# Choices sorted by expert number, early gathers of the lower rows, and a turned sequence ahead of two whole experts

## Chip, cores and metric

One core of one Trainium2 chip runs the kernel. The metric is the device time of one execution in microseconds; of the kernel before, three runs gave 588.18 us (median), 587.75 and 590.46 us.

## What is computed

The reference is a chain of two layers over 16 sequences of 256 tokens with 256 features, all in float32. Layer 0 (attention with a conditioning bias, then a top-1 mixture of 8 experts) fills the first half of the kernel and is not touched by the change. Layer 1 has two parts, and the change is in how they meet:

```python
scores = softmax(logits); topk_w, topk_idx = top_k(scores, 2)      # per token, 8 small experts
y_all = einsum('etm,emh->eth', leaky(x @ w_gate) * (x @ w_up), w_down)
y = (y_all[topk_idx] * topk_w[..., None]).sum(1) + shared_expert(x)
...
pooled = y.mean(axis=1); gates = softmax(top-2 of pooled @ gate_w.T + gate_b)   # per sequence, 8 experts
out = x + einsum('be,beso->bso', gates, gelu(einsum('bsd,eod->beso', y, expert_w) + expert_b))
```

## The kernel before

Only the second half matters here. It has three stages that hand over to one another.

**Choice tiles.** The 8192 pairs of token and chosen expert are sorted by expert into 71 tiles of 128 rows (`TILES2`), every expert starting on a new tile. POOL gathers a tile's token rows by an indirect DMA (`choice_rows`), PE turns, multiplies and turns back (`choice_in`, `choice_up`, `choice_turn`, `choice_down`, three tiles in flight), ACT and DVE empty the banks, and SP stores the result to the DRAM tensor `y2_dram` (the profile calls it `y_sorted`), counted by three semaphores `c_st`. In DVE's queue each turn of the loop over `TILES2 + LAG` holds a copy of the turned tile (L2856) and two products (L2860, L2862).

**Shared expert.** Behind the last tiles PE works off the last units of the shared expert (L1503, L1520) while the stores land.

**Sequences.** For each of the 16 sequences POOL gathers four blocks of 128 rows out of `y2_dram`: two halves (`NB` = 2) times the token's first and second choice, by the row numbers `pos_k_i`. All go through `gather_rows` (L917), and behind each stands `space()`, a memset that POOL waits for (L947). The destination `yk` has three buffers (`RT`), so the gathers of sequence b wait for the sum of sequence b-3. No gather may start until all 71 tiles are stored (`c_st`). DVE then adds the weighted rows to the shared result (`sum_choices`, four instructions of L2883), PE turns the sum (`turn_z`, L1642), ACT copies it and gets its pooled mean, PE multiplies it by the gate weights (`gate_logits`, L1656), DVE picks the two experts (`gates`, L2892 to L2898), and PE reads their numbers into registers (`experts_of`, a load of `d_top`). For each of the two experts PE issues a bias (`gated_bias`, L1663) and eight matmuls (two calls of `gated` with four instructions each, L1669); ACT applies gelu (L2032) and DVE weighs the result into `res` (L2915), which SP stores.

PE's order in that stage is written out in `gated_step`: turn sequence b, second half of sequence b-1's first expert, gate logits of b, all of b-1's second expert, then the numbers of b and the first half of its first expert. At the last sequence one half of the second expert is drawn ahead of the turn, and `last_choice` splits the end in two. DVE's own `gated_step` has the gate chain of b, then the first weighing of b-1, then the sum of b+1.

## Time and profile before

| | us |
|---|---|
| median of three runs | 588.18 |
| the profiled execution | 589.62 |
| its span in the profile | 587.9 |
| mean granted TensorE clock | 0.998 of full speed |
| PE busy | 558.1 (95%) |
| DVE busy | 321.1 (55%) |
| ACT busy | 243.1 (41%) |
| POOL busy | 233.9 (40%) |

Busy time is the sum of an engine's instructions over the whole span; the matmul row counts pipelined instructions, whose ends are modelled, so a busy PE isn't one at its peak. Which engine sets the end is read by stage: from the chain of waits, from the windows of the three stages, and from what stands behind "idle before" in the timeline.

### The profile page before, as it was taken

The page shows a single profiled execution, that of the slowest core. Times are in us where ns is not written, and L with a number is a line of the kernel's source. Part 1 is how long each engine was busy: PE and PEld are TensorE (multiplying, and loading weights), DVE is VectorE, ACT ScalarE, POOL GpSimd, SP SyncE. Part 2 cuts the span into 40 slices and gives each one's busy share as a digit, 9 for nine tenths or more (in the row PEclk, how much of TensorE's full clock was granted, in tenths as well). Part 3 has the DMA queues.
Part 4 walks back from the last instruction along what each step waited for, and adds up shares of the span by engine and source line. Part 5 has one row for each costly group of instructions (what it writes and reads, how often), then busy time and mean ns, then how long its engine had stood idle before and what let it go on. Part 6 is the DMA issues. An engine that isn't in the chain of part 4 may idle for free.

```text
span 587.9 us, 11468 instructions
## 1 busy us (share of the span) xinstructions
PE 558.1 (95%) x3816; PEld 463.4 (79%) x3816; DVE 321.1 (55%) x967; ACT 243.1 (41%) x670; POOL 233.9 (40%) x319
## 2 busy tenths in 40 slices
PE   7999999988999999999999989999999998998886
PEld 4788887744999999988888968888878887776664
DVE  3877758676322225733538754444444344666665
ACT  1555444660211111116544245555555454443432
POOL 2312211042111121007546365555555078777860
PEclk9999999999999999999999999999999999999999
DMA  5960000186995522513395035565655322444441
GB/s 149 387 284 4 1 1 2 64 366 254 325 345 191 184 68 73 153 64 74 76 308 191 0 100 148 160 159 150 161 153 153 96 78 85 136 129 121 127 134 56
DMA packets 48853, 83.96 MB, mean 143 GB/s; under 512 B 8946, under 2 KB 41587, under 8 KB 47252
## 3 DMA queue, kind: packets, MB, share of 16 engines
q1 hardware_dynamic: 40676, 60.97, 29.7%
q0 software_dynamic: 8112, 22.16, 15.5%
q8 instruction: 36, 0.59, 0.4%
q14 instruction: 29, 0.24, 0.1%
HBM read 62.25 MB, written 20.84 MB: 141 GB/s over the span
## 4 chain that ended last, share of the span: by engine, by line
PE 70%; POOL 12%; DVE 5%; issue 5%; DMA 4%; ACT 2%; another core or an unknown queue 0%; SPq 0%; POOLq 0%; DVEq 0%; ACTq 0%
POOL arena L917 10%; PE psum L1331 10%; PE psum L1344 9%; PE psum L1591 9%; PE psum L1503 7%; PE psum L1605 5%; PE psum L1187 5%; PE psum L1159 5%; PE psum L1520 3%; PE psum L1583 3%; DMA arena<-x,row_tok 3%; POOL iota_i L947 2%; PE psum L1167 2%; PE psum L1538 1%; PE psum L1181 1%
## 5 line engine op out<-in xcount | busy, mean ns | idle before, releaser
L917 POOL DMA_INDIRECT arena<-x,row_tok x71 | 68.1, 959 | 55.7 <-PE psum L1583 47.2
L917 POOL DMA_INDIRECT arena<-y_sorted,pos_k_i x64 | 65.3, 1021 | 35.2 <-issue 16.1
L1591 PE MATMUL psum<-big_w,arena 128*128 x284 | 72.9, 379 | 0.0
L1927 ACT ACTIVATE arena<-psum,arena 128x128 f32<-128x128 f32 x64 | 18.2, 368 | 106.5 <-PE psum L1331 85.0
L1669 PE MATMUL psum<-big_w,arena 128*128 x248 | 61.3, 379 | 0.0
L1331 PEld LDWEIGHTS psum<-arena,big_w 128*128 128x128 f32 x512 | 59.5, 192 | 1.7 <-issue 1.0
L1331 PE MATMUL psum<-arena,big_w 128*128 128x128 f32 x512 | 59.8, 275 | 0.8 <-DVE arena L2624 0.8
L1503 PE MATMUL psum<-arena,big_w 128*128 128x256 f32 x256 | 59.9, 381 | 0.2 <-ACT arena L1946 0.2
L1591 PEld LDWEIGHTS psum<-big_w,arena 128*128 128x128 f32 x284 | 53.7, 190 | 7.2
L1344 PE MATMUL psum<-arena 128*128 128x256 f32 (+1 forms) x256 | 57.7, 379 | 0.0
L2860 DVE SCALAR_TENSOR_TENSOR arena<-arena 128x128 f32<-128x128 f32 x71 | 20.8, 293 | 62.2 <-ACT arena L2013 62.2
L1503 PEld LDWEIGHTS psum<-arena,big_w 128*128 128x128 f32 x256 | 47.3, 190 | 7.1 <-ACT arena L1946 0.9
L1344 PEld LDWEIGHTS psum<-arena 128*128 128x128 f32 x256 | 47.5, 190 | 5.8
L1669 PEld LDWEIGHTS psum<-big_w,arena 128*128 128x128 f32 x248 | 45.7, 190 | 6.7
L917 POOL DMA_INDIRECT arena<-h_late,row_tok x16 | 15.3, 959 | 81.7 <-PE psum L1319 69.6
L1605 PE MATMUL psum<-big_w,arena 128*128 x142 | 44.1, 392 | 1.3 <-ACT arena L2010 1.3
L892 POOL TENSOR_TENSOR arena<-arena 128x512 f32<-128x512 f32 x16 | 19.0, 1191 | 59.9 <-DVE arena L2223 59.8
L2010 ACT COPY arena<-psum 128x256 f32<-128x256 f32 x71 | 26.4, 372 | 22.2 <-PE psum L1605 19.5
L1187 PE MATMUL psum<-arena 128*128 128x256 f32 x144 | 32.7, 380 | 0.4 <-ACT arena L1806 0.4
L1159 PE MATMUL psum<-arena 128*128 128x128 f32 x256 | 32.6, 289 | 0.0
L1520 PE MATMUL psum<-big_w,arena 128*128 128x256 f32 x128 | 30.6, 382 | 1.3 <-ACT arena L1950 1.3
L1159 PEld LDWEIGHTS psum<-arena 128*128 128x128 f32 x256 | 31.4, 204 | 0.3 <-DVE arena L2223 0.2
(338 smaller groups left out, 997.8 us busy)
## 6 DMA issues: line engine op xcount, KB each, us to landing
y_sorted<-arena SPq DMA_DIRECT2D x71, 128.0 KB
big_w<-w SPq DMA_DIRECT2D x8, 1024.0 KB, 5.3
tokens<-x SPq DMA_DIRECT2D x4, 1024.0 KB, 13.3
x<-tokens SPq DMA_DIRECT2D x16, 256.0 KB, 2.6
out<-arena SPq DMA_DIRECT2D x15, 256.0 KB
y_late<-arena SPq DMA_DIRECT2D x16, 128.0 KB, 1.7
big_w<-expert_w_t SPq DMA_DIRECT2D x1, 2048.0 KB, 7.4
arena<-x,row_tok POOLq DMA_INDIRECT x71
```

The source lines that it names most:

```text
L917: pool.indirect_dma_start(dst, None, rows, bass.IndirectOffsetOnAxis(ap=idx, axis=0)).then_inc(done, 16)
L1159: mm = pe.matmul(bank[a][:, (j % 4) * P:(j % 4 + 1) * P], wq_s[:, k, j * P:(j + 1) * P], xt_l[:, k, :], start=k == 0, stop=k == KD - 1)
L1187: mm = pe.matmul(bank[6][:, 0:D], lhs(j), wo_s[:, j, :], start=j == 0, stop=j == NPAIR - 1)
L1331: mm = pe.matmul(bank[1 + 2 * u + f // 4][:, (f % 4) * P:(f % 4 + 1) * P], big_w[:, c:c + P], g_t[u][:, k, :], start=k == 0, stop=k == KD - 1)
L1344: mm = pe.matmul(bank[5 + j % 2][:, 0:D], act_t[j % 2][:, f, :], arena[:, bass.ds(e * (NF * D) + f * D, D)], start=f == 0, stop=f == NF - 1)
L1503: mm = pe.matmul(bank[up_bank(b) + q][:, half * S:(half + 1) * S], w[:, k, q * M1:(q + 1) * M1], p_s[:, unit(b)[1][k], :], start=k == 0, s ...
L1520: mm = pe.matmul(bank[6][:, n * D:(n + 1) * D], mid[u][q][:, n * P:(n + 1) * P], md_s[:, E1 + q, :], start=q == 0, stop=q == NSH - 1)
L1591: mm = pe.matmul(bank[2 + i % RT][:, 0:2 * M1], c_gt[i % RT][:, k, :], mgu_s[:, k, bass.ds(e, 1), :].rearrange("p a m -> p (a m)"), start= ...
L1605: pe.matmul(bank[5][:, 0:D], c_midt[i % RT], md_s[:, bass.ds(e, 1), :].rearrange("p a d -> p (a d)"), start=True, stop=True).then_inc(c_dn, 1)
L1669: mm = pe.matmul(o, z_t[u][:, k, n * P:(n + 1) * P], ew_s[:, k, bass.ds(e, 1), :].rearrange("p a d -> p (a d)"), start=False, stop=n == NB ...
L2010: act.copy(c_y[t % RT], bank[5][:, 0:D]).then_inc(c_yc, 1)
L2860: dve.scalar_tensor_tensor(c_mid[v], c_leak[v], 0.01, c_leak[v], ALU.mult, ALU.max).then_inc(c_lkd, 1)
```

## The change

It has four parts.

1. **By expert number.** At tile 12 of the choice loop DVE runs `by_expert`, 14 small instructions. They order a token's two choices by row number (and so by expert number, since experts are stored one behind the other), rewrite `pos_k_i` and the weights `w_k` in that order, and work out how many tiles of each of the three store semaphores lie before the last expert's first tile.
2. **Lower rows early.** The lower row of a token never lies in the last expert's tiles. POOL waits, behind all its choice gathers, for the stores up to that expert only, and gathers the lower rows of the first five sequences (`y_lo`, 5 buffers). Then come the full wait and the higher rows of three sequences (`y_hi`, 3 buffers); from there on two blocks of higher rows of b and two of lower rows of b+2 alternate. There are 64 gathers as before.
3. **A turned sequence ahead.** PE's step now turns sequence c+1, reads the numbers of c, does all of its first expert, the gate logits of c+1, and all of its second expert. The special order at the last sequence goes, apart from `last_choice`. DVE's step sums sequence b+1 ahead of the gate chain of b.
4. **Filled destination.** SP copies 71 x 128 rows of x into `y2_dram` in three DRAM to DRAM transfers, queued behind the first load of the layer-0 weights, and waits for them before the first store of a choice tile.

The diff, cut to its core:

```diff
-        yk = [N.take(2 * NB, D) for _ in range(RT)]
+        y_hi = [N.take(NB, D) for _ in range(RT)]
...
+        NLO = 5
+        y_lo = [N.take(NB, D) for _ in range(NLO)]
...
+            def fill_choice():
+                for r0 in range(0, TILES2 * P, T):
+                    n = min(T, TILES2 * P - r0)
+                    sp.dma_start(y2_dram[r0:r0 + n, :], x[0:n, :]).then_inc(filled, 16)
...
                 sp.dma_start(big_w[:, :], w1).then_inc(ld_w1, 16)
+                fill_choice()
...
+            sp.wait_ge(filled, 16 * NFILL)
             for i in range(TILES2):
                 sp.wait_ge(c_yc, i + 1)
...
+            pool.wait_ge(table, 4)
+            for u in range(RT):
+                hold(pool, c_st[u], pool.value_load(stores_i[0:1, u:u + 1], min_val=16, max_val=16 * len(range(u, TILES2, RT))))
+            for b in range(NLO):
+                low_rows(b)
             for u in range(RT):
                 pool.wait_ge(c_st[u], 16 * len(range(u, TILES2, RT)))
+            for b in range(RT):
+                high_rows(b)
+            for b in range(RT, B):
+                pool.wait_ge(d_z, b - RT + 1)
+                high_rows(b)
+                if b + NLO - RT < B:
+                    low_rows(b + NLO - RT)
...
+            def gated_step(c):
+
+                u, v = c % RT, (c + 1) % RT
+                more = c + 1 < B
+                if more:
+                    turn_z(c + 1, v)
+                first, second = experts_of(c, u)
+                gated_bias(c, 0, first)
+                gated(c, u, 0, 0, first)
+                gated(c, u, 0, 1, first)
+                if more:
+                    gate_logits(c + 1)
+                    gated_bias(c, 1, second)
+                    gated(c, u, 1, 0, second)
+                    gated(c, u, 1, 1, second)
+                else:
+                    last_choice(c, u, second)
...
+            def by_expert():
+
+                for u in range(RT):
+                    g = dve.tensor_scalar(first_i[:, u:u + 1], tstart2[:, E1 - 1:E1], float(RT - 1 - u), 21846.0, ALU.add, ALU.mult)
+                link(dve.tensor_tensor(lower, pos_k[:, :, 0], pos_k[:, :, 1], ALU.is_lt))
+                link(dve.tensor_scalar(first_i, first_i, 16, None, ALU.logical_shift_right))
+                dve.tensor_copy(first_f, first_i)
+                link(dve.tensor_scalar(higher, lower, -1.0, 1.0, ALU.mult, ALU.add))
+                dve.tensor_scalar(stores_i[:, :], first_f, 1.0, 16.0, ALU.max, ALU.mult)
+                dve.tensor_tensor(pos_k_i[:, :, 0], pos_k[:, :, 0], pos_k[:, :, 1], ALU.min)
+                link(dve.tensor_tensor(pos_k_i[:, :, 1], pos_k[:, :, 0], pos_k[:, :, 1], ALU.max))
+                dve.sem_inc(table, 1)
+                dve.tensor_tensor(w_lo, w_k[:, :, :], lower.unsqueeze(1).broadcast_to([P, 2, NC]), ALU.mult)
+                link(dve.tensor_tensor(w_hi, w_k[:, :, :], higher.unsqueeze(1).broadcast_to([P, 2, NC]), ALU.mult))
+                dve.tensor_tensor(w_k[:, 0, :], w_lo[:, 0, :], w_hi[:, 1, :], ALU.add)
+                dve.tensor_tensor(w_k[:, 1, :], w_lo[:, 1, :], w_hi[:, 0, :], ALU.add)
+
+            SORT_AT = 12
...
+                if i == SORT_AT:
+                    by_expert()
...
+                if b + 1 < B:
+                    all_of(sum_choices(b + 1, (b + 1) % RT, (b + 1) // RT))
                 chain = gates(b, b % RT) if b < B else iter(())
                 for _ in range(3):
                     next(chain, None)
-                if 1 <= b:
-                    outs[b - 1] = weigh(b - 1, (b - 1) % RT, (b - 1) // RT)
-                    next(outs[b - 1])
-                if 1 <= b and b + 1 < B:
-                    all_of(sum_choices(b + 1, (b + 1) % RT, (b + 1) // RT))
+                outs[b - 1] = weigh(b - 1, (b - 1) % RT, (b - 1) // RT)
+                next(outs[b - 1])
                 next(chain, None)
```

**POOL, where the choice gathers end.** Before, the first gather of `y_sorted` waits for all three store semaphores:

```order
L917 DMA arena<-x,row_tok 128x256 [waits c_g] x64
L917 DMA arena<-y_sorted,pos_k_i 128x256 [waits c_st2,c_st1,c_st0]
L947 MEMSET iota_i 128x128
L917 DMA arena<-y_sorted,pos_k_i 128x256 [waits paced]
L947 MEMSET iota_i 128x128
```

Changed (here `gather_rows` is L937 and the memset L967):

```order
L937 DMA arena<-x,row_tok 128x256 [waits c_g] x64
L1020 TENSOR_LOAD stores_i [waits table]
L1020 ISA x2
L1020 TENSOR_LOAD stores_i [waits c_st0]
L1020 ISA x2
L1020 TENSOR_LOAD stores_i [waits c_st1]
L1020 ISA x2
L937 DMA arena<-y_sorted,pos_k_i 128x256 [waits c_st2]
L967 MEMSET iota_i 128x128
L937 DMA arena<-y_sorted,pos_k_i 128x256 [waits paced]
L967 MEMSET iota_i 128x128
```

Three reads of `stores_i` now stand there, each with a partial wait for a store semaphore behind it. Ten gathers with their memsets follow, and only then the wait for all stores (`c_st1,c_st2,c_st0,paced`) that stood alone before.

**PE, one step of the sequence stage.** Before (L1642 turns, L1669 is an expert's matmuls, L1663 a bias, L1656 the gate logits, L1311 the load of the expert numbers; the ISA rows set up addresses):

```order
L1311 TENSOR_LOAD d_top [waits d_ok]
L1663 ISA [waits d_ge]
L1663 MATMUL psum<-big_w,ones_bf 128x512
L1669 ISA
L1669 MATMUL psum<-big_w,arena 128x256
L1669 ISA
L1669 MATMUL psum<-big_w,arena 128x256
L1642 MATMUL psum<-ident,arena 128x128 [waits d_ztc,d_z]
L1642 MATMUL psum<-ident,arena 128x128 x3
L1669 MATMUL psum<-big_w,arena 128x256 x2
L1656 MATMUL psum<-big_w,arena 128x8 [waits d_log,d_ztc]
```

Changed (the same four are L1675, L1702, L1696 and L1689, the load L1344):

```order
L1675 MATMUL psum<-ident,arena 128x128 [waits d_ztc,d_z]
L1675 MATMUL psum<-ident,arena 128x128 x3
L1344 TENSOR_LOAD d_top [waits d_ok]
L1696 ISA [waits d_ge]
L1696 MATMUL psum<-big_w,ones_bf 128x512
L1702 ISA
L1702 MATMUL psum<-big_w,arena 128x256
L1702 ISA
L1702 MATMUL psum<-big_w,arena 128x256 x3
L1689 MATMUL psum<-big_w,arena 128x8 [waits d_log,d_ztc]
```

The load of the numbers has moved behind the turn of the next sequence, and between the turn and the gate logits there are now the bias and all four matmuls of an expert instead of two matmuls (each counts as two instructions in the profile, so eight and four there).

**DVE, one step of the sequence stage, changed.** L2918 is the sum, L2927 to L2933 the gate chain, L2950 the weighing:

```order
L2918 SCALAR_TENSOR_TENSOR arena<-arena,w_k 128x256 [waits a_dc,d_lo4,d_zt]
L2918 SCALAR_TENSOR_TENSOR arena<-arena,w_k 128x256
L2918 SCALAR_TENSOR_TENSOR arena<-arena,w_k 128x256 [waits d_z1,c_got1]
L2918 SCALAR_TENSOR_TENSOR arena<-arena,w_k 128x256
L2927 SCALAR_TENSOR_TENSOR arena<-psum,arena 128x8 [waits d_lg]
L2930 MAX arena<-arena 128x8 [waits d_log]
L2933 MAX_INDEX d_top<-arena 128x8 [waits d_sub]
L2950 SCALAR_TENSOR_TENSOR arena<-arena,tokens 128x512 [waits d_gt,d_ge]
```

The sum stood behind the first weighing and waited once, for four gathers; it now stands ahead of the gate chain and waits for the lower rows first and for the higher rows (`c_got`) in its middle.

## Rows read from the trace of the kernel before

**Rows 1.** The page: the chain that ended last, by engine and by line.

```profile
PE 70%; POOL 12%; DVE 5%; issue 5%; DMA 4%; ACT 2%; another core or an unknown queue 0%; SPq 0%; POOLq 0%; DVEq 0%; ACTq 0%
```

**Rows 2.** Windows of sequence stage: stretch, length, busy per engine, clock, DMA share, GB/s.

```profile
core 0: us, PE busy (x) PEld busy (x) DVE busy (x) ACT busy (x) POOL busy (x), PEclk, DMA share, GB/s
499.00:575.00 76.00, 68.27 (x344) 51.83 (x344) 50.27 (x161) 31.29 (x104) 56.48 (x91) 1.00 0.42 125
```

**Rows 3.** Timeline of POOL: start, duration, instruction, idle before; the gathers' end.

```profile
454.93 0.94 POOL L917 DMA_INDIRECT arena<-x,row_tok  x1 [0.73 <-PE psum L1583]
470.87 0.94 POOL L917 DMA_INDIRECT arena<-y_sorted,pos_k_i  x1 [15.00 <-DMA y_sorted<-arena]
471.82 0.22 POOL L947 MEMSET iota_i<- 128x128 int32 x1
472.31 0.95 POOL L917 DMA_INDIRECT arena<-y_sorted,pos_k_i  x1 [0.27 <-POOL iota_i L947]
...
501.17 0.95 POOL L917 DMA_INDIRECT arena<-y_sorted,pos_k_i  x1 [0.27 <-POOL iota_i L947]
...
569.24 0.98 POOL L917 DMA_INDIRECT arena<-y_sorted,pos_k_i  x1 [0.27 <-issue]
```

**Rows 4.** The chain in order of time: from a gather to the sum.

```profile
563.37 2.66 DMA arena<-y_sorted,pos_k_i
```

**Rows 5.** Timeline, the first two sums and PE's first expert.

```profile
478.91 1.79 DVE L2883 SCALAR_TENSOR_TENSOR arena<-arena,w_k 128x256 f32<-128x256 f32 x4
490.24 1.82 DVE L2883 SCALAR_TENSOR_TENSOR arena<-arena,w_k 128x256 f32<-128x256 f32 x4
492.68 0.10 PEld L1663 LDWEIGHTS psum<-big_w,ones_bf 128*128 128x128 bf16 x1
```

**Rows 6.** Timeline of PE and its weight loads, one step.

```profile
558.64 0.38 PE L1663 MATMUL psum<-big_w,ones_bf 128*128 x1
560.58 0.38 PE L1663 MATMUL psum<-big_w,ones_bf 128*128 x1
562.50 0.42 PEld L1642 LDWEIGHTS psum<-ident,arena 128*128 128x128 f32 x4 [1.07 <-DVE arena L2883]
564.08 0.52 PEld L1656 LDWEIGHTS psum<-big_w,arena 128*128 128x128 f32 x4 [0.46 <-ACT arena L2019]
564.55 0.38 PE L1663 MATMUL psum<-big_w,ones_bf 128*128 x1
```

**Rows 7.** One choice tile on DVE and PE.

```profile
422.96 0.28 DVE L2856 COPY arena<-psum 128x128 f32<-128x128 f32 x1
423.78 0.30 PEld L1605 LDWEIGHTS psum<-big_w,arena 128*128 128x128 f32 x2
```

**Rows 8.** Timeline of DVE: small instructions in a chain, and two without a wait.

```profile
311.78 0.16 DVE L2795 TENSOR_SCALAR cnt_i<-arena 128x8 int32<-128x8 f32 x1
312.80 0.42 DVE L2800 SCALAR_TENSOR_TENSOR arena<-arena 128x256 f32<-128x256 f32 x1
...
315.53 0.65 DVE L2805 TENSOR_SCALAR arena<-pos_k_i 128x64 int32<-128x64 int32 x1
```

**Rows 9.** SP's issues and landing time of the first weight load; what follows on the queue.

```profile
13.59 1.44 SPq L721 DMA_DIRECT2D big_w<-w  x1
111.23 0.29 SPq L725 DMA_DIRECT2D h_late<-arena  x1
big_w<-w SPq DMA_DIRECT2D x1, 28.0
```

**Rows 10.** Window between the first weight load and the next transfer, columns as in Rows 2.

```profile
45.00:111.00 66.00, 64.27 (x726) 52.84 (x725) 48.74 (x102) 33.57 (x69) 10.92 (x10) 1.00 0.01 2
```

**Rows 11.** The load of the expert numbers: duration ns min/median/max.

```profile
L1311 PEldq TENSOR_LOAD <-d_top x16: 532/534/547, 491.1 to 577.9; - x16
```

**Rows 12.** Timeline of the end, on PE and DVE.

```profile
574.80 0.57 PEld L1642 LDWEIGHTS psum<-ident,arena 128*128 128x128 f32 x4
577.19 0.17 DVE L2892 SCALAR_TENSOR_TENSOR arena<-psum,arena 128x8 f32<-128x8 f32 x1 [2.29 <-PE psum L1656]
577.67 0.16 DVE L2898 FIND_INDEX8 d_top<-arena 128x8 uint32<-128x8 f32 x1
578.57 0.10 PEld L1663 LDWEIGHTS psum<-big_w,ones_bf 128*128 128x128 bf16 x1 [0.86 <-issue]
```

More of the change, by code:

```diff
@@ L408, in bass_adaln_ffn_kernel @@
         tile_f2 = Q.take(TILES2)
+        first_i = Q.take(RT).bitcast(I32)
+        first_f = Q.take(RT)
+        stores_i = sb("stores_i", [P, RT], I32)
+        lower = Q.take(NC)
+        higher = Q.take(NC)
+        w_lo = Q.take(2, NC)
+        w_hi = Q.take(2, NC)
         NLB = NU // 4
         lgt_2 = Q.take(S)
+        assert N.at <= E0 * NF * D + Q.at
         wt_g = router_g
@@ L534, in bass_adaln_ffn_kernel @@
         d_back = sem("d_back")
-        d_pos = sem("d_pos")
         d_log = sem("d_log")
@@ L553, in bass_adaln_ffn_kernel @@
         c_st = [sem(f"c_st{k}") for k in range(3)]
-        d_got = [sem(f"d_got{k}") for k in range(3)]
+        d_lo = [sem(f"d_lo{k}") for k in range(NLO)]
+        filled = sem("filled")
         d_st = [sem(f"d_st{k}") for k in range(3)]
@@ L567, in bass_adaln_ffn_kernel @@
         half_st0 = 16 * len(range(0, TILES2, RT))
-        last_got = c_got[0:2]
-        last_got0 = [16 * len(range(u, TILES2, RT)) for u in range(2)]
+        d_hi, d_hi0 = c_got, [16 * len(range(u, TILES2, RT)) for u in range(RT)]
+        NFILL = -(-TILES2 * P // T)
         l_rows_ev, l_beat_g, ld_rest = ld_x[2], ld_x[1], ld_x[3]
@@ L721, in _ @@
                 sp.dma_start(big_w[:, :], w1).then_inc(ld_w1, 16)
+                fill_choice()
                 late_rows = h_late[1:, :].rearrange("(c p) d -> p c d", p=P)
@@ L1732, in _ @@
                 shared_down(s, s % 2)
-            first_expert(0, 0)
-            for b in range(1, B + 1):
-                gated_step(b)
+            for c in range(B):
+                gated_step(c)
             def every_expert(b, first):
@@ L2868, in sum_choices @@
                     hold(dve, d_zt, b - RT + 1)
-                split = isinstance(b, int) and b == B - 1
-                if split:
-                    dve.wait_ge(last_got[0], last_got0[0] + 32)
-                else:
-                    hold(dve, d_got[u], 64 * turn_no + 64)
+                dve.wait_ge(d_lo[b % NLO], 32 * (b // NLO) + 32)
                 if isinstance(b, int):
```

59 lines of the change are left out of this document (17 added, 42 removed).

## The prediction

> **What bounds the kernel now.** I read the chain of waits first, then the windows, then the timelines of the stage that the change is in. Over the whole span the chain lies 70% on PE and 12% on POOL [rows 1]. POOL's part is one stage: with the choice tiles done, each sequence costs four gathers, and in the window of the sequences POOL is busy 56.48 of 76 us though nothing it does is long [rows 2]. The timeline of POOL says why: a gather takes 0.95 us, then comes a memset of 0.22 and 0.27 of hand-over, so the next one starts 1.44 us later (472.31 behind 470.87) at best. All 64 run from 470.87 to 569.24 + 0.98 = 570.22, 99.35 us or 1.55 each [rows 3]. Four are 6.2 us per sequence.
>
> PE needs less. In one step the bias and eight matmuls of an expert take 560.58 - 558.64 = 1.94 us, the four transposes about 0.42, the gate logits 564.55 - 564.08 = 0.47 [rows 6]. Two experts, a turn and the logits: 4.8 us. The step takes 564.55 - 558.64 = 5.91, and the rest stands in the same rows as idle time: 1.07 us for DVE's sum, which waits for gathers, and 0.46 for ACT's copy of the turned sequence [rows 6]. So gathers bound the stage, PE stands a good microsecond behind. Ahead of it POOL is idle for 15.00 us, from its last choice gather to the landing of the last store [rows 3].
>
> **The sum, part by part,** in the time of the profiled execution (589.62, of which 587.9 is the span).
>
> *Fill.* 71 x 128 rows of 1 KB are 9.3 MB. The transfers stand behind a load of 8.4 MB that is issued at 13.59 and needs 28.0 us, 0.30 MB per us; at that rate the fill ends near 42 + 31 = 73. SP's next transfer is issued at 111.23 [rows 9], and in between the DMA engines are at 0.01 [rows 10]. Cost 0: the cover is 38 us of spare time. No row shows a DRAM to DRAM copy. Were each byte counted twice (read and written) at the same rate, it would end at 42 + 62 = 104, still in time; that is why I take 0, with a rival below for less.
>
> *by_expert.* 14 instructions of 32 to 64 elements per partition or fewer. Five small chained ones take 312.80 - 311.78 = 1.02 us, 0.20 each [rows 8]. Six of the 14 are waited for (6 x 0.20), the others overlap and start about 0.1 apart: 2.0 us, and I take 2.3. If every one cost what the slow one of the same chain does, 0.65 [rows 8], it would be 9; if they fell into DVE's gaps, 0. In the tile loop PE is the bound, and what queues behind the block on DVE is the copy of a turned tile, done at 422.96 + 0.28 = 423.24 while PE begins its matmul at 423.78 [rows 7]. That leaves 0.54 us of cover, so PE loses 2.3 - 0.54 = 1.8 us, once, and nothing later gives it back. **+1.8.**
>
> *Lower rows early.* Ten gathers at 1.45 need 14.5 us and fit in the hole of 15.00, if the partial wait is over by then. It is: counting the reference's choices for these inputs gives 69 used tiles, of which the last expert has the last 11, so POOL waits for tile 57, stored some ten tiles ahead of 455.9. At 470.87 POOL goes on with six gathers of higher rows (to about 480), then with the first block of two and two behind the sum of sequence 0, done at 478.91 + 1.79 = 480.7 [rows 5]; by 487 it has issued 20. Now a new wait comes: the next block needs the sum of sequence 1, which DVE's order puts at 490.24 + 1.82 = 492.06 [rows 5]. So POOL stands idle for 5 us, and the head start isn't ten gathers: gather 21 starts at 492.2 instead of 501.17 [rows 3]. That idle time also means that the early gathers may be 5 us late for nothing. From gather 21 on POOL waits for nothing (its next waits are for sums three sequences back), and the remaining 44 take what the last 44 take now, 570.22 - 501.17 = 69.05 us [rows 3]. They end at 561.3. **-8.9.**
>
> *PE's new order.* PE's first expert starts at 492.7 as before [rows 5]. At 4.85 us a step PE would begin the turn of sequence 15 at 492.7 + 14 x 4.85 = 560.6; the gathers are later, so they still decide at the end. A gather lands 2.66 us after its start [rows 4], 1.7 after its end; with DVE's queue I take 2.1. The higher rows of sequence 14 are complete two gathers ahead of the last (558.2), land at 560.3, and the two halves of the sum that wait for them take 0.9: 561.2. The turn comes at 561.4. Then a wait that wasn't there: DVE has the gate chain of 13 behind this sum (577.83 - 577.19 = 0.64 us [rows 12]), PE loads the numbers (0.53 [rows 11]), and starts the expert's weights 578.57 - 577.83 = 0.74 after the chain [rows 12]: 562.7, though the turn was done at 561.9. Expert, logits, expert: 562.7 + 1.94 + 0.47 + 1.94 = 567.05, where sequence 15 (summed by 564.4) is turned. Today the turn comes at 574.80 [rows 12], 4.6 us behind the last gather; then it is 5.8 behind. **+1.2.**
>
> *The end.* Behind the turn of sequence 15 PE now has eight matmuls and two biases more (10 x 0.215 = 2.15 us), since nothing is drawn ahead; two waits go, 0.46 for the copy, as in every step [rows 6], and 0.86 for the numbers [rows 12]. **+0.9.**
>
> Sum: 1.8 - 8.9 + 1.2 + 0.9 = -5.0, so 584.6 for the profiled execution. The median is 1.44 lower than that execution, and the predicted median is 588.18 - 5.0 = **583.2**.
>
> *Rule:* the time of the load that moved behind the turn is a row here, 0.53 us from SBUF. The Trainium skill (Runtime: NRT & Kernel Launch, The launch sequence) gives 1.3 us for such a load from HBM; by that figure the one exposed load would add 0.8 and the median be 584.0. The trace's 0.53 decides.
>
> **Rivals.**
> 1. *PE becomes the bound.* The pace of 1.55 holds stretched gathers; the plain pace is 1.44, and 44 x 1.44 = 63.4 us ends at 555.6. Then PE's floor of 560.6 for the last turn decides, 6.4 earlier than above: 576.8. For it: most gathers do take 0.95. Against: DVE's sums stay as dense as now. Halfway is likelier than the whole: 577 to 580.5. Chance 0.17.
> 2. *The numbers come late in every step.* DVE now sums b+1 ahead of the gate chain of b. If sums wait for gathers throughout, each step has the 0.8 us wait: 14 x 5.65 = 79.1, last turn at 571.8, 4.7 later than above, a median of 587.9. It decides from the point where the gathers have no lead over PE. Against: POOL starts three to five sequences ahead and loses about 1.3 us a step, so the lead lasts past half of the stage. Chance 0.14.
> 3. *Slower: the fill is still running at 111.* It decides below 9.3 MB in 69 us, 0.135 MB per us, under half the rate of the load ahead. SP's stores of the attention result then stand behind it, and PE's next work behind them; at 0.10 MB per us the end is 135, 24 us late, less 5 gained: 607. Against: 64 rows of 64 KB, the row length of that load. Chance 0.04.
> 4. *DVE's block costs 9 us* (upper bound above), PE 8.5: 589.9. Chance 0.04.
> 5. *The early gathers do nothing,* because the partial wait is as late as the full one. POOL then ends as before, and the new order alone gives +1.8 + 1.2 + 0.9: 592. Chance 0.03.
>
> **How the numbers follow.** The forecast has 0.58; its own bounds (block 0.5 to 3, gathers 1.45 to 1.62) reach from 579 to 587. A measurement tells apart some 0.5%, 2.9 us. Faster by more: nearly all of the forecast (0.56), rival 1 (0.17) and a little of rival 2 (0.03), 0.76. Within 0.5%: the rest of these two and half of rival 4, 0.15. Slower: 0.09. The range reaches down through most of rival 1 and up through rival 2: 578.0 to 588.3.
>
> **What would show it.** Right: ten gathers of `y_sorted` between 456 and 472 in the shifted time; POOL idle for some 5 us ahead of gather 21; PE steps near 4.85 us with no wait for the copy in the first half, near 6 in the last; the wait for numbers only there; one gap of near 1.8 us on PE around tile 12; no stretch ahead of 111 longer. Wrong: idle time ahead of the bias in every step (rival 2), POOL waiting for `d_z` throughout (rival 1), a late store at 111 (rival 3).

## The result and the profile after

The changed kernel takes 590.25 us (median of 19 runs, 587.65 to 596.55); the kernel before, on the same chip, 587.75 (19 runs). The ratio is 1.006, interval 1.0041 to 1.0079: slower by 0.6%, where 0.8% faster was forecast. Ratios, here and below, are taken over all runs of both kernels, so they aren't exactly those of the medians; and since the kernel before takes 586.27 to 590.46 us by the chip, only ratios compare runs of different chips. The profiled executions are 593.32 and 589.62, spans 591.6 and 587.9, so 3.7 us are to be found.

From the page of the changed kernel, the clock and traffic in 40 slices of 14.8 us, and the chain that ended last [rows 1]:

```profile
PEclk9998899999999999999999999999999999999999
...
GB/s 149 389 423 353 135 2 1 2 206 428 190 330 269 191 139 52 137 113 47 90 185 336 6 45 144 136 156 160 159 161 161 150 126 55 115 144 131 119 117 56
...
PE 72%; POOL 9%; DVE 7%; issue 5%; DMA 4%; ACT 1%; SPq 1%; POOLq 0%; DVEq 0%; ACTq 0%
```

POOL's share of the chain fell from 12% to 9%, as it should. But "issue", an engine that waits for nothing the profile shows, stands at 5%, and PE's clock is below 0.9 in slices 4 and 5 alone, the last two with the fill's traffic. So the program has to be cut into stages, at marks that both kernels have: SP's store of the attention result, POOL's last choice gather, its last gather, the end.

| stretch | before | after | difference | forecast |
|---|---|---|---|---|
| start to attention store | 111.23 | 120.45 | +9.2 | 0 |
| to the last choice gather | 343.70 | 343.55 | -0.2 | +1.8 |
| to the end of the last gather | 115.29 | 107.59 | -7.7 | -8.9 |
| to the end of the span | 17.68 | 20.01 | +2.3 | +2.1 |

The loss lies in the first stretch, hundreds of microseconds ahead of anything that the change was about. Only the fill is new there. SP's timeline of the changed kernel and, from the view of transfers, issue to landing:

```profile
15.19 1.85 SPq L698 DMA_DIRECT2D y_sorted<-x  x3
...
120.45 0.29 SPq L744 DMA_DIRECT2D h_late<-arena  x1
```

```profile
y_sorted<-x SPq DMA_DIRECT2D x1, 896.0 KB, 52.2
...
y_sorted<-x SPq DMA_DIRECT2D x2, 44.2
```

The fill has landed by 15.19 + 1.85 + 52.2 = 69 us at the latest, earlier than the 73 that I gave it; nothing queues behind it. PE's timeline, before and changed, and the windows of that stretch (columns as in [rows 2]):

```profile
17.50 0.69 PE L1167 MATMUL psum<-arena 64*64 64x65 f32 x32 [0.69 <-ACT arena L1839]
...
53.08 0.69 PE L1167 MATMUL psum<-arena 64*64 64x65 f32 x32 [0.73 <-issue]
```

```profile
16.51 0.70 PE L1200 MATMUL psum<-arena 64*64 64x65 f32 x32 [0.88 <-DVE arena L2312]
...
56.21 1.15 PE L1200 MATMUL psum<-arena 64*64 64x65 f32 x32 [4.86 <-issue]
...
58.83 1.93 PE L1214 MATMUL psum<-arena 64*64 64x512 f32 x8
...
66.33 1.58 PE L1192 MATMUL psum<-arena 128*128 128x128 f32 x12 [2.22 <-issue]
```

The first of these windows is the kernel before, the other three are the changed one:

```profile
50.00:55.00 5.00, 4.26 (x85) 3.35 (x87) 1.19 (x3) 2.07 (x5) 0.00 (x0) 1.00 0.02 7
```

```profile
50.00:55.00 5.00, 1.35 (x11) 1.02 (x9) 0.00 (x0) 1.45 (x3) 0.00 (x0) 0.90 1.17 397
55.00:60.00 5.00, 3.79 (x74) 2.44 (x74) 2.52 (x4) 1.01 (x3) 0.16 (x1) 0.50 1.11 341
45.00:111.00 66.00, 58.63 (x669) 48.45 (x667) 39.03 (x72) 26.75 (x55) 10.71 (x9) 0.92 0.30 100
```

PE stands idle for 4.86 and 2.22 us with no semaphore to blame. At the first place the kernel before waits too, but 0.73 us. Behind the changed kernel's wait the clock is at 0.50, the 1.2 GHz level, and the eight matmuls of L1214 take 1.93 us, 1.04 elsewhere. Idle time is (4.86 - 0.73) + 2.22 = 6.4 us. The slow clock costs more than the 2.8 that this leaves of the 9.2: PE was 1.0 us ahead at the start (16.51 for 17.50), and from where PE resumes to the store it takes 120.45 - 56.21 = 64.2 us where the kernel before takes 111.23 - 53.08 = 58.1, so 6.1 more, of which 2.22 is the second wait. The slow clock is the other 3.9: 6.4 + 3.9 - 1.0 is 9.2 but for rounding. The last row answers to [rows 10]: 669 matmul records in place of 726.

What is PE waiting for? The DMA view lists a queue that I had passed over, the one that brings instructions. Cut to 0.2 us (columns: packets, MB, share of 16 engines), it shows one block of 0.02 MB (16 KB) at a time. Before, at 50.4, and after, at 53.2:

```profile
q8 instruction: 1, 0.02, 29.0%
```

```profile
q1 hardware_dynamic: 2, 0.13, 193.9%
q8 instruction: 1, 0.02, 34.6%
```

The block itself takes hardly longer (29% and 35% of 16 x 0.2 us, some 1 us). It is later, and PE goes on 2.7 to 3.0 us behind it in both: 50.4 to 53.08, 53.2 to 56.21. The second wait has its block too: the changed kernel's next one is at 63.6, and PE goes on at 66.33, 2.7 us behind. The view doesn't say whose instructions q8 brings; that these blocks are PE's is concluded from this distance, which all profiles below have. The Trainium skill (Runtime: NRT & Kernel Launch, Instruction fetch mechanics) says that a sequencer fetches its program in 16 KiB blocks over a DMA queue of its own, at a cost "mostly hidden". The trace agrees on the block and its queue; hidden it is in the kernel before, but for 0.73 us, and not here.

The late stages, POOL first:

```profile
466.61 0.95 POOL L937 DMA_INDIRECT arena<-y_sorted,pos_k_i  x1 [1.66 <-DMA y_sorted<-arena]
...
494.82 0.95 POOL L937 DMA_INDIRECT arena<-y_sorted,pos_k_i  x1 [0.27 <-issue]
...
501.84 0.99 POOL L937 DMA_INDIRECT arena<-y_sorted,pos_k_i  x1 [5.85 <-DVE arena L2918]
...
570.64 0.95 POOL L937 DMA_INDIRECT arena<-y_sorted,pos_k_i  x1 [0.27 <-issue]
```

The partial wait costs 1.66 us where the full one cost 15.00 [rows 3], twenty gathers are out by 495.8, POOL then stands for 5.85 us, and the last 44 take 69.75. PE's weight loads, with the idle time ahead of them:

```profile
374.84 0.14 PEld L1632 LDWEIGHTS psum<-ident,arena 128*128 128x128 f32 x1 [1.58 <-issue]
...
506.36 0.58 PEld L1675 LDWEIGHTS psum<-ident,arena 128*128 128x128 f32 x4
...
511.05 0.58 PEld L1675 LDWEIGHTS psum<-ident,arena 128*128 128x128 f32 x4
...
545.93 0.42 PEld L1675 LDWEIGHTS psum<-ident,arena 128*128 128x128 f32 x4 [2.14 <-DVE arena L2918]
547.18 0.10 PEld L1696 LDWEIGHTS psum<-big_w,ones_bf 128*128 128x128 bf16 x1 [0.82 <-issue]
...
572.33 0.42 PEld L1675 LDWEIGHTS psum<-ident,arena 128*128 128x128 f32 x4 [1.98 <-DVE arena L2918]
573.57 0.10 PEld L1696 LDWEIGHTS psum<-big_w,ones_bf 128*128 128x128 bf16 x1 [0.82 <-issue]
577.62 0.58 PEld L1675 LDWEIGHTS psum<-ident,arena 128*128 128x128 f32 x4
```

There is the gap behind by_expert (1.58, or 1.37 counted in PE's matmuls), steps of 4.69 us with no wait in the first half, and from 545.9 on five steps that wait for gathers and then 0.82 for the numbers.

### The profile page after: what moved, and what is told of

It reads as the page before. It is cut to its first block, busy times and chain, and to the rows that moved or that the text cites. A ratio compares the mean times of both kernels' runs of the same rounds, so it can differ in the third digit from the quotient of the medians.

```text
span 591.6 us, 11515 instructions
## 1 busy us (share of the span) xinstructions
PE 556.2 (94%) x3816; PEld 467.4 (79%) x3816; DVE 321.6 (54%) x981; ACT 240.7 (41%) x670; POOL 232.3 (39%) x319
## 4 chain that ended last, share of the span: by engine, by line
PE 72%; POOL 9%; DVE 7%; issue 5%; DMA 4%; ACT 1%; SPq 1%; POOLq 0%; DVEq 0%; ACTq 0%
PE psum L1364 10%; PE psum L1377 9%; PE psum L1536 9%; PE psum L1624 9%; POOL arena L937 8%; PE psum L1220 5%; PE psum L1638 5%; PE psum L1192 4%; PE psum L1553 4%; PE psum L1616 3%; DMA arena<-x,row_tok 2%; PE psum L1200 2%; POOL iota_i L967 2%; PE psum L1702 1%; PE psum L1571 1%
## 5 line engine op out<-in xcount | busy, mean ns | idle before, releaser
L937 POOL DMA_INDIRECT arena<-x,row_tok x71 | 68.1, 958 | 55.5 <-PE psum L1616 45.9
L937 POOL DMA_INDIRECT arena<-y_sorted,pos_k_i x64 | 64.9, 1014 | 28.0 <-issue 13.8
L1624 PE MATMUL psum<-big_w,arena 128*128 x284 | 72.9, 379 | 0.0
L1702 PE MATMUL psum<-big_w,arena 128*128 x248 | 58.6, 379 | 0.0
L1702 PEld LDWEIGHTS psum<-big_w,arena 128*128 128x128 f32 x248 | 46.6, 189 | 5.9
L937 POOL DMA_INDIRECT arena<-h_late,row_tok x16 | 15.4, 960 | 81.7 <-PE psum L1352 69.5
L1638 PE MATMUL psum<-big_w,arena 128*128 x142 | 44.6, 396 | 0.0
L2918 DVE SCALAR_TENSOR_TENSOR arena<-arena,w_k 128x256 f32<-128x256 f32 x64 | 28.1, 480 | 15.9 <-DMA arena<-y_sorted,pos_k_i 14.9
L1220 PE MATMUL psum<-arena 128*128 128x256 f32 x144 | 34.4, 394 | 0.4 <-ACT arena L1826 0.4
```

The lines of the kernel that those rows point to most:

```text
L937: pool.indirect_dma_start(dst, None, rows, bass.IndirectOffsetOnAxis(ap=idx, axis=0)).then_inc(done, 16)
L1220: mm = pe.matmul(bank[6][:, 0:D], lhs(j), wo_s[:, j, :], start=j == 0, stop=j == NPAIR - 1)
L1624: mm = pe.matmul(bank[2 + i % RT][:, 0:2 * M1], c_gt[i % RT][:, k, :], mgu_s[:, k, bass.ds(e, 1), :].rearrange("p a m -> p (a m)"), start= ...
L1638: pe.matmul(bank[5][:, 0:D], c_midt[i % RT], md_s[:, bass.ds(e, 1), :].rearrange("p a d -> p (a d)"), start=True, stop=True).then_inc(c_dn, 1)
L1702: mm = pe.matmul(o, z_t[u][:, k, n * P:(n + 1) * P], ew_s[:, k, bass.ds(e, 1), :].rearrange("p a d -> p (a d)"), start=False, stop=n == NB ...
L2918: m = dve.scalar_tensor_tensor(z_s[u][:, n, :], (y_hi[u] if k else y_lo[b % NLO])[:, n, :], w_k[:, k, bass.ds(b * NB + n, 1)], base, ALU.m ...
```

## The experiments

The theory: the fill holds back the fetch of PE's instructions. Its rivals: the loss is elsewhere; or the traffic as such slows PE.

**e1, the fill alone in the kernel before.**

```diff
                 sp.dma_start(big_w[:, :], w1).then_inc(ld_w1, 16)
+                fill_choice()
...
+            sp.wait_ge(filled, 16 * NFILL)
             for i in range(TILES2):
```

> The kernel before with the fill alone: the same three transfers issued behind the first weight load, SP waiting for them ahead of the first choice store. Theory A (the fill costs what the change lost, and nothing else was mispriced): the gap between 48 and 67 us appears here too, +9.3 us, 597 by the measurement's median of 587.75, ratio 1.016. Theory B (the loss comes from the choice and sequence stages, and the stretched attention stage of the profiled run was an accident): no change, 587 to 589.

Measured: 597.94, ratio 1.0109 (1.0058 to 1.0161). PE waits 6.65 us at the same place, the store comes at 118.75, 7.5 us late. Theory B has fallen: the fill alone makes a loss of that kind. By the ratio it is 6.4 us of 590.46, where 9.3 was expected; PE waits once here, and twice in the changed kernel.

**e2, the change without the fill.** The lower rows are read from 59 of the 71 tiles, which is enough for these inputs.

```diff
-                fill_choice()
...
-                    gather_rows(y_lo[b % NLO][:, n, :], y2_dram, ...)
+                    gather_rows(y_lo[b % NLO][:, n, :], y2_dram[0:59 * P, :], ...)
```

> The changed kernel without the fill (the lower rows are read from the first 59 of the 71 tiles only, which the partial wait covers for these inputs). Theory A: attention as before, 9.3 us off the 590.25 of the changed kernel, so 581 to 583, ratio 0.991 to the kernel before. Theory B: 590 as with the fill.

Measured: 585.97, ratio 0.9913 (0.9884 to 0.9941). Of the 590.46 of the kernel before on that chip the ratio makes 5.1 us, the two medians are 4.5 apart; -5.0 was forecast.

**e3 and e5, the fill in pieces of 4 KB.** e3 puts pairs in the outer dimension (a = 2), e5 sixteen.

```diff
-                    sp.dma_start(y2_dram[r0:r0 + n, :], x[0:n, :]).then_inc(filled, 16)
+                    sp.dma_start(y2_dram[r0:r0 + n, :].rearrange("(b a r) d -> a b (r d)", a=16, r=4),
+                                 x[0:n, :].rearrange("(b a r) d -> a b (r d)", a=16, r=4)).then_inc(filled, 16)
```

> The changed kernel, the same bytes of fill cut into pieces of 4 KB in place of 64 KB. Theory A1 (a block of PE's instructions that is fetched stands behind the fill's long packets on its DMA engine): PE's wait for nothing shown at 51 and 64 us shrinks to under 1 us and the clock stays at 1.00, the total near 582 to 584. Theory A2 (the number of bytes moved, by its share of the memory or by the clock, slows PE): the same loss, 589 to 591, with a clock of 0.5 somewhere while the fill runs.

> The changed kernel, the fill in pieces of 4 KB again, now interleaved over 16 so that all DMA engines carry them, and the bytes move about as fast as in the change (over 250 GB/s between 42 and 70 us). The third run moved 4 KB pieces at 54 GB/s only, over few engines, so it told long packets from short ones at unlike rates. Theory A1 (a fetched block of PE's instructions stands behind long packets): the block that was fetched at 49.8 without the fill and at 53.2 with it is fetched within 0.5 us of its time, PE's wait at 52 is near 1 us, clock 1.00, and the total 582 to 586 if the fill is over by 111. Theory A2 (bytes per us, whatever their packets): the wait of 4 to 6 us and the clock of 0.5 are back, 589 to 592.

Measured, e3: 686.42, ratio 1.1609 (1.1548 to 1.167). SP's timeline and one window tell why:

```profile
15.68 171.40 SPq L698 DMA_DIRECT2D y_sorted<-x  x3
```

```profile
55.00:65.00 10.00, 10.00 (x118) 9.14 (x120) 6.79 (x14) 5.35 (x11) 2.38 (x2) 1.00 0.14 54
```

Issuing takes SP until 187, at 54 GB/s and a share of 0.14 of 16 DMA engines, some two of them. The Trainium skill (DMA: Bandwidth & Descriptors, Why a DMA increments its semaphore by 16 and not by 1) says that a transfer is spread over the largest number up to 16 that divides the sizes of its outermost dimension: two here, as the trace shows. This was my own edit's trap, and by accident it is rival 3 of the prediction, SP's store stuck behind the fill, at 96 us. PE lost nothing in attention up to there (wait 0.74, clock 1.00), but at so low a rate that tells nothing of packets. Hence e5: 587.72, ratio 1.003 (1.0006 to 1.0054). PE's timeline and the windows:

```profile
54.97 1.14 PE L1201 MATMUL psum<-arena 64*64 64x65 f32 x32 [3.90 <-issue]
```

```profile
50.00:55.00 5.00, 1.10 (x13) 0.86 (x11) 0.00 (x0) 1.45 (x3) 0.00 (x0) 0.89 1.03 324
55.00:60.00 5.00, 5.00 (x76) 2.94 (x77) 3.69 (x6) 1.69 (x4) 1.20 (x1) 0.50 1.02 324
```

At full rate short pieces hold the fetch back as well (it stands at 52.0), and PE waits 3.90 us. The idea that only long packets do it has fallen; whether they add something (4.86 us for 3.90), one profile of each doesn't tell.

**e4 and e6, the fill paced**, in 512 and in 1024 rows, one transfer at a time.

```diff
-                for r0 in range(0, TILES2 * P, T):
+                for j, r0 in enumerate(range(0, TILES2 * P, FR)):
+                    sp.wait_ge(filled, 16 * j)
...
                 sp.dma_start(big_w[:, :], w1).then_inc(ld_w1, 16)
+                sp.wait_ge(ld_w1, 16)
                 fill_choice()
```

> The changed kernel, the same bytes in 18 transfers of 512 rows, each issued when the one ahead has landed, the first when the weight load has. Packets keep their kind but few are queued at a time (512 KB over 16 engines). Theory A1: each engine has one packet of the fill ahead of a fetch at most and idle time between transfers, so the waits of PE are under 1 us, total 582 to 584; the fill ends before 111. Theory A2: as many bytes over some 70 us in place of 25: a third of the loss per us for three times as long, so most of the loss stays, 587 to 591.

> The changed kernel, nine transfers of 1024 rows, each issued when the one ahead has landed: 64 KB for each of 16 DMA engines at a time, where the fourth run had 32 KB. Theory A1: a fetch stands behind at most one packet that is under way, 64 KB at some 25 GB/s, 2.6 us, so PE's wait at 52 is anywhere from 1 to 3.5 us, total 583 to 588. If several queued packets had to go first whatever the pacing (A1b), it would be as in the fourth run. Theory A2: a loss by the bytes, 587 to 591.

Measured: e4 587.05, ratio 0.9931 (0.9902 to 0.9959), PE's wait 1.32; e6 587.69, ratio 1.0013 (0.9984 to 1.0042), PE's wait 2.60. In the window 50 to 55 the DMA engines are at 0.61 (213 GB/s) in e6; in e4 at 0.36 (109 GB/s) from 45 to 55. By its ratio e4 would take 587.75 x 0.9931 = 583.7 on the first chip, in the range of theory A1. By these three (e4, e6, e5) the block is later, the more of the DMA engines' time the fill takes. Two more runs say that the share alone doesn't settle it. e8 and e10, further down, have e4's paced pieces. In e8 PE waits 1.25 us with a share of 0.65 in the window 50 to 55; in e10 it waits 2.19 with 0.36, and the clock falls behind it:

```profile
53.31 0.70 PE L1202 MATMUL psum<-arena 64*64 64x65 f32 x32 [2.19 <-issue]
```

What the block meets just when it is due may decide; no run separates that.

**e9, the same fill later.** One wait is added, nothing else:

```diff
                 sp.dma_start(big_w[:, :], w1).then_inc(ld_w1, 16)
+                sp.wait_ge(o_ps, 4)
                 fill_choice()
```

> The changed kernel with its fill as it is (three transfers, long packets, full rate), issued when the fourth product of attention is done, at about 63 us in place of 15. Without the fill PE's blocks are fetched at 41, 49.8, 53, 57, then 68, 78, 89 and 99 us, and only behind the fetch of 49.8 does PE wait. Theory A3 (what the fill delays is the fetch of instructions, by some 3 us while it keeps all DMA engines busy, and that costs only where PE has used up its blocks): from 63 to some 90 us three fetches come late and PE waits for none of them, clock 1.00, the total as without a fill, ratio 0.991 to 0.994. Theory A2' (the fill's traffic slows PE or takes its clock wherever it lies): a loss of 5 to 9 us stays, ratio 1.002 to 1.01.

Measured: 583.41, ratio 0.9896 (0.9856 to 0.9937), clock 1.000 over the span. The windows ahead of the fill and during it:

```profile
42.00:63.00 21.00, 20.09 (x203) 17.21 (x194) 15.52 (x29) 9.45 (x20) 4.76 (x4) 1.00 0.01 3
63.00:93.00 30.00, 30.00 (x390) 25.33 (x389) 21.29 (x39) 16.28 (x35) 6.50 (x6) 1.00 0.94 311
```

PE is busy for all of the 30 us in which the fill runs at 311 GB/s. The blocks do come late (71.4, 84.4 and 93.0 us, without a fill 68.4, 78.6 and 89.0), and PE waits for none. This settles it: the traffic neither slows PE nor takes its clock; it delays fetches, here by 3 to 6 us, and that costs only where three blocks follow each other (49.8, 53, 57): there the changed kernel waits twice, the others of the table once. My reading is that PE has no block in hand there. It goes with the windows: the kernel before has 85 matmuls between 50 and 55, and 38 between 45 and 50. No run shows how many blocks PE holds.

**e13, a load into SBUF in the fill's place.** The first weights are loaded twice; no fill, lower rows as in e2.

```diff
                 sp.dma_start(big_w[:, :], w1).then_inc(ld_w1, 16)
+                sp.wait_ge(ld_w1, 16)
+                sp.dma_start(big_w[:, :], w1).then_inc(ld_w1, 16)
```

> The second run's kernel (no fill) that loads the first weights a second time, 8.4 MB from HBM to SBUF in 64 KB rows, issued when they have landed the first time: from 44 to some 70 us. Theory A4 (any transfer that keeps all 16 DMA engines busy holds back the fetch, whatever its ends): PE's wait at 52 is 3 to 6 us, clock 0.5 behind it, 588 to 592 in all, ratio 1.000 to 1.006. Theory A5 (only a copy from HBM to HBM does it): the wait stays near 1 us, the clock at 1.00, ratio 0.991.

Measured: 589.4, ratio 1.0015 (0.9986 to 1.0044). PE's timeline and the windows:

```profile
56.00 1.15 PE L1199 MATMUL psum<-arena 64*64 64x65 f32 x32 [4.02 <-issue]
```

```profile
50.00:55.00 5.00, 1.99 (x14) 1.57 (x12) 0.00 (x0) 1.45 (x3) 0.00 (x0) 1.00 0.99 423
55.00:60.00 5.00, 4.00 (x75) 2.48 (x75) 2.71 (x4) 1.22 (x3) 0.36 (x1) 0.66 0.97 419
```

An ordinary weight load does the same. The kernel before has one from 14 to 42, with a DMA share of 0.88 between 25 and 40; two blocks are fetched under it, at 22.4 and 34.6, and PE waits for neither, as in e9. It is the time of the transfer that matters, not its kind.

All of it in one table. "Fetch" is the window of 0.2 us that holds the block, "resumes" PE's next matmul, "DMA" the share in the window 50 to 55 (45 to 55 in e1 to e4, 42 to 63 in e9), "clock" that of the window 55 to 60 (55 to 65 in e1 to e4). "Late" corrects for the start, which differs by up to 1.8 us between profiles: it is the block's distance from PE's stop at 16 to 18 us (17.50 before), less 32.93. In the six profiles without a bulk transfer around 50 us whose clock is full at the start (before, e2, e9, e11, e12, e14) that distance is 32.92 to 32.95 (e7, also without one, has 33.55 behind a start with a clock of 0.57 from 18 to 22):

| kernel | DMA | fetch | late | resumes | PE idle | clock | store |
|---|---|---|---|---|---|---|---|
| before | 0.02 | 50.4 | 0.0 | 53.08 | 0.73 | 1.00 | 111.23 |
| e2 none | 0.01 | 49.8 | 0.0 | 52.83 | 1.02 | 1.00 | 110.97 |
| e9 later | 0.01 | 49.8 | 0.0 | 52.77 | 0.91 | 1.00 | 110.92 |
| e3 4 KB, narrow | 0.14 | 49.4 | 0.0 | 52.20 | 0.74 | 1.00 | 187 |
| e4 512 rows | 0.36 | 49.8 | 0.5 | 52.70 | 1.32 | 1.00 | 110.86 |
| e8 512 rows | 0.65 | 49.6 | 0.5 | 52.27 | 1.25 | 1.00 | 110.42 |
| e10 512 rows | 0.36 | 50.6 | 1.4 | 53.31 | 2.19 | 0.75 | 113.02 |
| e6 1024 rows | 0.61 | 51.0 | 1.5 | 54.16 | 2.60 | 0.66 | 113.90 |
| e5 4 KB, wide | 1.03 | 52.0 | 2.9 | 54.97 | 3.90 | 0.50 | 115.69 |
| e13 reload | 0.99 | 53.2 | 3.3 | 56.00 | 4.02 | 0.66 | 115.62 |
| after | 1.17 | 53.2 | 3.9 | 56.21 | 4.86 | 0.50 | 120.45 |
| e1 fill alone | 0.95 | 55.0 | 5.7 | 57.87 | 6.65 | 0.55 | 118.75 |

PE resumes 2.7 to 3.2 us behind the block in all twelve. From there to the store it takes 58.1 to 58.2 us where the clock stays at 1.00 (e3 aside, whose store stands behind the fill), and 59.6 to 60.9 where it falls once (e6, e10, e5, e13, e1). So a fall of the clock costs 1.5 to 2.7 us, on top of the wait.

**e7, the lower rows late**, on e2's base: both waits stand ahead of the first lower row.

```diff
+            for u in range(RT):
+                pool.wait_ge(c_st[u], 16 * len(range(u, TILES2, RT)))
             for b in range(NLO):
                 low_rows(b)
```

> The second run's kernel (no fill) with POOL's two waits ahead of the first lower rows, so that these ten gathers follow the landing of the last store. My reading of the change: the ten gathers then start some 14 us later, POOL is never idle behind them, and the last gather ends 8 to 9 us later, so does the kernel: 586 + 8.5 = 594, ratio 1.007. Rival (the early rows are worth little, since POOL stands idle for 5.85 us behind them anyway, and the order of PE's and DVE's work gives what the second run gained): under 3 us, 586 to 589.

Measured: 594.3, ratio 1.0114 (1.0071 to 1.0158); e2's is 0.9913. From POOL's timeline and PE's:

```profile
471.11 1.16 POOL L934 DMA_INDIRECT arena<-y_sorted,pos_k_i  x1 [15.24 <-DMA y_sorted<-arena]
...
571.58 0.95 POOL L934 DMA_INDIRECT arena<-y_sorted,pos_k_i  x1 [0.27 <-issue]
```

```profile
574.75 3.40 PE L1699 MATMUL psum<-big_w,arena 128*128 x8
578.00 0.51 PE L1686 MATMUL psum<-big_w,arena 128*128 128x8 f32 x4
578.57 1.89 PE L1699 MATMUL psum<-big_w,arena 128*128 x8
```

The wait of 15 us is back, the last gather starts at 571.58 where e2 has it at 562.49, 9.1 us later, as the term of 8.9 says. The rest of the 10.6 us between the two spans (594.3 and 583.7) shows in the second fence: an expert's matmuls at the lower clock, 3.40 us for 1.89, behind waits of 1.43 and 0.59. By the two ratios the loss is 2.0%, more than the 8 to 9 us expected. The rival (under 3 us) has fallen.

**e8, eight buffers for lower rows** (with e4's paced fill; three buffers in free columns of big_w).

```diff
-        NLO = 5
-        y_lo = [N.take(NB, D) for _ in range(NLO)]
+        NLO = 8
+        y_lo = [N.take(NB, D) for _ in range(5)] + [X.take(NB, D) for _ in range(NLO - 5)]
```

> The fourth run's kernel (paced fill) with eight buffers for lower rows in place of five, three of them in a free part of big_w. POOL has 26 gathers to issue ahead of its wait for the sum of sequence 1 in place of 20: the idle time of 5.85 us in front of gather 21 goes, and the last gather ends 5.8 us earlier. If the gathers bound the end: 587 - 5.8 = 581.3, ratio 0.984. Rival (PE takes over as the bound halfway, at 4.68 us a step from its first expert): the last turn comes no earlier than 14 steps behind the first, a gain of 3 to 6 all the same. Rival (gathers stretch where they meet the sums on DVE): a gain under 2 us.

Measured: 581.05, ratio 0.9907 (0.988 to 0.9934). The last gather starts at 554.30, 7.6 us ahead of e4's 561.90, but the kernel got some 1.5 us of it by the two ratios, where 5.8 and a ratio of 0.984 were forecast. PE's timeline:

```profile
485.79 0.66 PE L1677 MATMUL psum<-ident,arena 128*128 128x128 f32 x4 [3.14 <-DVE arena L2920]
...
540.46 0.66 PE L1677 MATMUL psum<-ident,arena 128*128 128x128 f32 x4 [1.11 <-DVE arena L2920]
541.71 0.39 PE L1698 MATMUL psum<-big_w,ones_bf 128*128 x1 [0.59 <-ACT arena L2054]
```

The first higher row now stands behind 16 gathers, and PE waits 3.14 us for the sum of sequence 0; in the middle PE runs out of higher rows while POOL collects lower ones that nobody needs yet. The idle time of POOL was gone; that the order of its work had become the bound is my reading, which e14 tests.

**e10, e11, e12: three edits on e8.** e10 cuts by_expert at its waits into six pieces, one per tile from 12 to 17 on; e11 adds e9's later fill; e12 also puts DVE's gate chain of b ahead of the sum of b + 1 from b = 6 on.

```diff
                 link(dve.tensor_tensor(lower, pos_k[:, :, 0], pos_k[:, :, 1], ALU.is_lt))
+                yield
...
-                if i == SORT_AT:
-                    by_expert()
+                if i >= SORT_AT:
+                    next(sort, None)
```

> The eighth run's kernel with by_expert cut at its waits into six pieces, one behind each tile from 12 to 17 on. The block cost PE 1.4 to 1.6 us in one place; a piece takes 0.2 to 0.6, below the 0.5 to 0.7 that DVE has to spare in a tile. Expected: 1.0 to 1.5 us less than the eighth run (ratio 0.9907 there), 0.988 to 0.989. Rival: each piece pushes its tile by a little, no gain.

> The tenth run's kernel with the fill unpaced and issued at 63 us as in the ninth, in place of 18 paced pieces from 42 us on. Theory A3: as the tenth or up to 0.5 us less, since PE's wait at 52 goes from 1.3 to 1.0. Theory A2': 5 us or more slower than the tenth.

> The eleventh run's kernel with DVE's gate chain of b ahead of the sum of b + 1 from b = 6 on, as the kernel before has it. In the eighth run PE lost some 3.5 us between 534 and 548, to a sum that waited for gathers and to what stands behind it. If the chain behind the late sum is what PE misses there, 0.5 to 1.5 us less than the eleventh; if the gathers are, no change; if the chain waits for PE's logits and holds the sum back, up to 1 us more.

Measured on one chip: e10 584.99, ratio 0.9904 (0.9869 to 0.9938); e11 584.2, ratio 0.9886 (0.9841 to 0.9932); e12 587.38, ratio 0.9957 (0.9934 to 0.998). e10's 0.9904 is outside the 0.988 to 0.989 expected. The pieces do hide: in e12 PE has no wait above 0.15 us between 362 and 390, where e9 has one of 1.00. But the stretch from the attention store to the last choice gather varies from 342.8 to 345.9 us between profiles (e3 aside), so 1 to 1.5 us can't be seen in the total: inconclusive. e11 against e10: the later fill is no worse in the total, more can't be told there; in the profiles e11's store is at 110.21, e10's at 113.02, PE's wait at 52 to 53 being 0.91 and 2.19. e12 is clear, and the other way: a wait in each of its nine late steps, all but one of 0.54 to 0.55 like these of PE's timeline,

```profile
559.35 0.65 PE L1676 MATMUL psum<-ident,arena 128*128 128x128 f32 x4 [0.55 <-DVE arena L2925]
565.02 0.66 PE L1676 MATMUL psum<-ident,arena 128*128 128x128 f32 x4 [0.54 <-DVE arena L2925]
```

5.67 us apart, 1 us over the plain step. What PE waits for is the sum, as the third of the three expectations had it: with the gathers early, the chain that waits for PE's logits holds back the sum. The order of the change is right there.

**e14, five buffers for higher rows and six for lower**, the fill as in e9.

```diff
-            for b in range(RT, B):
-                pool.wait_ge(d_z, b - RT + 1)
+            for b in range(NHI, B):
+                pool.wait_ge(d_z, b - NHI + 1)
                 high_rows(b)
-                if b + NLO - RT < B:
-                    low_rows(b + NLO - RT)
+                if b + NLO - NHI < B:
+                    low_rows(b + NLO - NHI)
```

> The changed kernel with the fill at 63 us as in the ninth run, and eleven gather buffers as in the eighth but six for lower and five for higher rows. In the eighth run the first higher rows came behind 16 gathers of lower ones, so PE waited 3.14 us for the sum of sequence 0 and its first expert started 4 us later than in the ninth; and all lower rows were gathered a step early, so PE ran out of higher ones at 534 to 548. Now the first sum waits for 14 gathers, and the higher rows of sequence 10 are gather 44 in place of 52. Theory (PE is never behind the gathers then): first expert at 493, 4.68 us a step to the end, last turn near 558 to 559 in place of 566: 572 to 576 in the profile, ratio 0.975 to 0.98. Rival (gathers at 1.5 us still reach the last step late): last turn at 561 to 563, ratio 0.982 to 0.986.

Measured: 576.71, ratio 0.9808 (0.9772 to 0.9843), the best of all and 1.9% below the kernel before. POOL's last gather, and four of PE's rows:

```profile
553.21 0.95 POOL L940 DMA_INDIRECT arena<-y_sorted,pos_k_i  x1 [0.27 <-issue]
```

```profile
492.03 0.60 PE L1678 MATMUL psum<-ident,arena 128*128 128x128 f32 x4
...
534.17 0.60 PE L1678 MATMUL psum<-ident,arena 128*128 128x128 f32 x4
...
540.15 0.39 PE L1699 MATMUL psum<-big_w,ones_bf 128*128 x1 [0.45 <-issue]
...
561.47 0.60 PE L1678 MATMUL psum<-ident,arena 128*128 128x128 f32 x4
```

As many buffers as in e8, gathers that end 1 us earlier, and the turn ahead of the first expert at 492.03 in place of 496.67. Nine steps take (534.17 - 492.03) / 9 = 4.68 us each, as forecast. Then come one of 4.9 and three of 5.9 with short waits, of which the row at 540.15 is one: 0.4 for the numbers, 0.3 for the copy. The last is plain again. So the last turn is at 561.47, in the range of the rival, and the ratio lies between my two cases: the gathers still reach PE a little late, for three steps.

## Why the prediction was wrong, and where it was right

**The step that failed is the fill: "Cost 0: the cover is 38 us of spare time."** It measured 9.2 us between the profiles, in a stretch that the sum had at nothing. I took as its cover that the DMA engines do nothing between 42 and 111, and asked only what SP issues next. The size of the fill, its rate and its end were right (69 us at the latest for 73). But "DMA at 0.01" in [rows 10] isn't nothing: it is PE's own program arriving in blocks of 16 KB, at 2 GB/s. What the runs showed in place of the spare time: under the fill a block comes 3.9 us late, PE stands idle for 6.4 us more, and the clock that falls behind the waits costs 3.9. The cover had a user, and this user was on the critical path at 50 us, as the 0.73 us of idle time with no releaser had shown in the trace of before. None of the rivals has it: rival 3 looked at the right transfer and at the wrong one who waits; e3 shows what it would have been.

**by_expert, +1.8:** PE's gap is 1.58, and its weight loads have gaps of 0.2 to 0.4 in that stage before, so some 1.4. The block takes 2.09 us on DVE, 2.3 was forecast. In the total it can't be seen.

**Lower rows early, -8.9:** -7.7 between the profiles, 9.1 by e7 against e2. Twenty gathers and then idle time, as forecast; POOL stood 5.85 us for 5, and the last 44 took 69.75 for 69.05.

**PE's new order and the end, +1.2 and +0.9:** 2.3 measured for both. The turn of sequence 15 comes 577.62 - 571.59 = 6.0 us behind the last gather (5.8 forecast), the end 14.0 us behind that turn. PE's plain step takes 4.69, not 4.85; while gathers decide at the end, that changes nothing. The numbers were waited for in the gather-bound half alone, so rival 2 was right for five steps in fourteen. Rival 1 came near only in e14, where the gathers hardly bind.

Without the fill the sum stands: -5.0 forecast, e2 -5.1 (0.9913 of 590.46). By the profiles, e2's four stretches differ from the kernel before's by -0.3, +1.3, -7.8 and +2.6, where 0, +1.8, -8.9 and +2.1 were forecast. The parts stand within some 1 us, but profiles of the second stretch differ by 3 us among themselves, so that the sum comes out within 0.1 is luck. With the fill, -5.0 + 9.2 = +4.2, and the profiles say +3.7. What stays open is why a fetch comes late. The Trainium skill (DMA: Bandwidth & Descriptors, Queues, rings and completion order) says that a DMA engine takes turns between its queues, a packet at a time; pieces of 4 KB and of 64 KB gave waits of 3.90 and 4.86 us here, and blocks 2.9 and 3.9 us late, and no run showed how a fetch is queued.

## What to carry to other kernels

Before calling a bulk transfer free because the DMA engines are idle, look for who else uses them: find PE's idle times with releaser "issue", and the instruction queue's blocks around them. Put such transfers where those waits are not (e9: one added wait on a semaphore, 1.6% of the time), or pace them, which is less sure (PE's wait was 1.32, 1.25 and 2.19 us in three kernels with the same pieces). Not every wait with releaser "issue" is a fetch: the 0.82 us ahead of the bias are the load of the numbers. When a queue of gathers bounds a stage, count for each consumer how many gathers stand ahead of its last one: e11 and e14 have the same eleven buffers and the same fill, and 0.8% lies between them (0.9886 and 0.9808, on two chips, with intervals that just meet). The order of the gathers is the main difference; the other, by_expert in pieces, is e11's, and was expected to help it.
